# First layer's full self attention: f32 score products in four 32-row bands instead of bf16 parts in stacks, with the closing stage inside

## What is computed

```python
def attention(x, w_qkv, b_qkv, w_o, b_o):       # 16 heads, dh = 8, no mask
    qkv = x @ w_qkv + b_qkv
    q, k, v = jnp.split(qkv, 3, axis=-1)
    ...
    scores = jnp.einsum('bqhd,bkhd->bhqk', q, k) / jnp.sqrt(jnp.float32(dh))
    probs = jax.nn.softmax(scores, axis=-1)
    ctx = jnp.einsum('bhqk,bkhd->bqhd', probs, v).reshape(B, T, D)
    return ctx @ w_o + b_o
h = x + attention(layer_norm(x, ln1_w, ln1_b), w_qkv, b_qkv, w_o, b_o)
return h + moe_ff(layer_norm(h, ln2_w, ln2_b), w_gate, w1, b1, w2, b2)
```

## Time and profile before

| | us |
|---|---|
| median of 3 runs | 2156.8 |
| profiled execution | 2162.13 |
| its span | 2160.4 |
| TensorE busy | 1709.4 (79%) |
| VectorE busy | 1297.4 (60%) |
| ScalarE busy | 1013.1 (47%) |
| mean granted TensorE clock | 0.893 |

### The profile page before, as it was taken

The page is one execution under the profiler, slowest core; times in us unless marked ns, Lnnn a source line. Parts: engine busy times, 40 slices in busy tenths (PEclk is TensorE's granted clock), DMA queues, the critical chain, the costliest instruction groups (busy, mean ns, idle before and its releaser), DMA issues. The chain is left out here.

```text
span 2160.4 us, 32545 instructions
## 1 busy us (share of the span) xinstructions
PE 1709.4 (79%) x9889; PEld 969.6 (45%) x9942; DVE 1297.4 (60%) x4106; ACT 1013.1 (47%) x1938; POOL 153.7 (7%) x280
## 2 busy tenths in 40 slices
PE   4187877287416955969999499999999989989997
PEld 2044444154201321336777344454545455656664
DVE  7388896565735844733333487767676745764445
ACT  3188884075103633643334167667576643332221
POOL 2000000300100000010000100000000002330000
PEclk8599998598756987988999799999999998998999
DMA  1533400340152124001000110000000000000000
GB/s 56 81 40 40 44 0 3 57 56 8 41 81 31 20 26 44 1 3 40 20 20 10 39 40 1 1 1 1 1 1 1 1 1 3 1 1 23 22 15 27
DMA packets 57630, 48.74 MB, mean 23 GB/s; under 512 B 12692, under 2 KB 53048, under 8 KB 57528
## 3 DMA queue, kind: packets, MB, share of 16 engines
q1 hardware_dynamic: 57527, 47.45, 13.8%
HBM read 38.30 MB, written 8.91 MB: 22 GB/s over the span
## 5 line engine op out<-in xcount | busy, mean ns | idle before, releaser
L557 DVE TENSOR_REDUCE c_NM<-ps_t 128x1 f32<-128x512 f32 x256 | 169.9, 688 | 96.9 <-PE ps_t L437 95.2
L1556 ACT ACTIVATE d_PT<-ps_t 128x512 f32<-128x512 f32 x256 | 150.5, 589 | 105.8 <-PE ps_t L1472 105.8
L1547 ACT ACTIVATE d_PR<-d_PR,d_NM 128x512 f32<-128x512 f32 x256 | 183.9, 718 | 32.9 <-DVE d_NM L1618 32.9
L437 PE MATMUL ps_t<-KX,QX 96*128 (+1 forms) x256 | 108.3, 428 | 105.6 <-DVE c_IB L575 46.8
L619 ACT ACTIVATE c_PT<-ps_s 128x1024 f32<-128x1024 f32 x128 | 130.4, 1024 | 126.6 <-PE ps_s L460 124.5
L2358 DVE SCALAR_TENSOR_TENSOR X<-ps_t,GATE,X 128x128 f32<-128x128 f32 x272 | 76.6, 344 | 185.3 <-PE ps_t L2283 185.3
L762 ACT ACTIVATE a_PR<-a_PR,a_NM 128x128 f32<-128x128 f32 (+3 forms) x256 | 129.8, 555 | 78.8 <-DVE a_NM L743 78.8
L1618 DVE CUSTOM_DVE_ANT_0 d_PR<-ps_s,d_BH 128x512 f32<-128x512 f32 x256 | 165.4, 683 | 0.3 <-PE ps_s L1463 0.2
L672 PE MATMUL ps_t<-ident,a_PR 128*128 128x128 f32 x640 | 117.9, 295 | 49.8 <-ACT a_PT L686 37.4
L2320 ACT ACTIVATE f_HT<-ps_s,f_BE 128x512 f32<-128x512 f32 x128 | 87.9, 687 | 128.6 <-PE ps_s L2273 127.8
L1463 PE MATMUL ps_s<-d_K,d_Q 64*128 64x512 f32 x512 | 145.0, 644 | 1.3 <-DVE d_NM L1618 1.3
(11 more groups left out here) (330 smaller groups left out, 2989.8 us busy)
## 6 DMA issues: line engine op xcount, KB each, us to landing
QX<-split_parts SPq DMA_DIRECT2D x108, 128.0 KB
KX<-split_parts SPq DMA_DIRECT2D x72, 128.0 KB
f_W<-in_L_ffn_w SPq DMA_DIRECT2D x16, 256.0 KB, 3.1
split_parts<-a_PARTS SPq DMA_DIRECT2D x8, 384.0 KB, 10.3
split_parts<-c_PARTS SPq DMA_DIRECT2D x8, 384.0 KB, 10.6
g_W<-in_L_ffn_w SPq DMA_DIRECT2D x24, 128.0 KB, 2.3
split_parts<-b_PARTS SPq DMA_DIRECT2D x4, 384.0 KB, 10.7
X<-in_x SPq DMA_DIRECT2D x4, 256.0 KB
```

Source lines behind the costliest of these rows:

```text
L437: nc.tensor.matmul(c.ps_t[:, i % 2, :], QX[0:SROWS, bass.ds(head, 1), qt * P:(qt + 1) * P], KX[0:SROWS, bass.ds(head, 1), :], start=True, ...
L557: nc.vector.tensor_reduce(NM[:, qt, j:j + 1], c.ps_t[:, i % 2, :], AX.X, ALU.max, negate=True).then_inc(maxed, 1)
L1547: nc.scalar.activation(PR[:, n % RING, e, :], PR[:, n % RING, e, :], ACT.Exp, scale=-1.0, bias=NM[:, n % RING, e:e + 1], accum_out=DEN[:, ...
L1556: nc.scalar.activation(PT[:, g % 2, e, :, qt * P:(qt + 1) * P], c.ps_t[:, e, :].rearrange("p (k q) -> p k q", q=P), ACT.Copy).then_inc(tak ...
```

## The change

The three blocks become one. The bf16 parts, their way through HBM, the stacks and the split of the maxima are gone. `NarrowWeights` loads all weights of the stage in seven DMAs, issued at the start of the closing block of the cross attention before it (`early`).

- Weights: queries' and keys' weights are copied into padded tiles in which each head has 32 columns (8 of its own, the rest zero), so that a projection of a group of four heads puts head j on rows 32j to 32j+7, its band. Row 32j+8 of the keys is one (from the bias), and the same row of the queries takes the negated maxima.
- Projections: queries and keys of step t+2 are computed in f32 within step t, values of the next batch in the first step of a batch, all through the one bank ps_f, whose users follow one another in the order of `shared_uses`.
- Scores: `score` contracts 8 rows of a band in f32 into one of three banks; VectorE takes the maxima, 24 tiles ahead of the rest. The 16 columns of maxima of a step are turned by one transpose, copied by ScalarE to 16 rows and written by four DMAs to the four rows 32j+8 of the queries.
- `score_by_key` contracts 9 rows of a band into one of three other banks, with the head two bands away from that of the `score` beside it; exp takes 512 columns; the four value products follow every fourth tile.
- The closing stage of a batch (context turned, output product, residual, statistics, normalised, turned back) runs inside the next batch's steps.
- All loops are written out; there is no hardware loop. The ones written into KX (L1141) are gone.

The diff, cut to its core; the lines removed from the old function are those printed above.

```diff
-def narrow_full_attention(c, tag, own, QX, KX, scratch, s_qx):
...
+    def load(self, sp, w, b, wo, bo, ln_w, ln_b):
+        sp.dma_start(self.W[:, :, :], w.rearrange("p (i n) -> p i n", i=3)).then_inc(self.loaded, 16)
+        sp.dma_start(self.BROW[:, :, :].rearrange("a i n -> a (i n)"), row(b, 1)).then_inc(self.loaded, 16)
+        sp.dma_start(self.BV[:, :], row(b[2 * P:3 * P])).then_inc(self.loaded, 16)
+        sp.dma_start(self.WO[:, :], wo).then_inc(self.loaded, 16)
+        sp.dma_start(self.BO[:, :], row(bo)).then_inc(self.loaded, 16)
+        sp.dma_start(self.WB[:, 0:1], col(ln_w)).then_inc(self.loaded, 16)
+        sp.dma_start(self.WB[:, 1:2], col(ln_b)).then_inc(self.loaded, 16)
...
+def narrow_full_attention(c, tag, weights, early=None):
...
+    MAXIMA_LEAD = 24
+    ALL = STEPS * TILES
+    MBANKS = [c.ps_s[:, i, :] for i in range(3)]
+    KBANKS = [c.ps_s[:, 3, :], c.ps_t[:, 0, :], c.ps_t[:, 1, :]]
+    PTS = 3
...
+        def shared_uses():
+
+            order = [("q", 0), ("k", 0), ("v", 0), ("q", 1), ("k", 1), ("n", 0)]
+            for t in range(STEPS):
+                b, g = divmod(t, GROUPS)
+                if t + 2 < STEPS:
+                    order += [("q", t + 2), ("k", t + 2)]
+                if t:
+                    order.append(("t", t - 1))
+                if t + 1 < STEPS:
+                    order.append(("n", t + 1))
+                if g == 0 and b + 1 < B:
+                    order.append(("v", b + 1))
+                if g and b:
+                    order.append((("1", "o", "x")[g - 1], b - 1))
+            order += [("t", STEPS - 1), ("1", B - 1), ("o", B - 1), ("x", B - 1)]
+            return dict(zip(order[1:], order))
...
+                for u in range(STEPS):
+                    sp.wait_ge(s_nm, u + 1)
                     for j in range(GH):
+                        sp.dma_start(QG[CW * j + HD8:CW * j + HD8 + 1, u % 3, :].rearrange("a (k q) -> a k q", q=P),
+                                     NMT[j * QT:(j + 1) * QT, u % 2, :]).then_inc(s_row, 16)
+                sp.wait_ge(s_row, rows_all * STEPS)
...
+                nc.gpsimd.memset(WP[:, :, :, :], 0.0).then_inc(s_zero, 1)
+                nc.gpsimd.memset(BP[:, :, :, :], 0.0).then_inc(s_zero, 1)
+                nc.gpsimd.memset(ONE[:, :], 1.0).then_inc(s_zero, 1)
+                pool.wait_ge(s_zero, 2)
+                nc.gpsimd.memset(BP[:, 1, :, HD8:HD8 + 1], 1.0).then_inc(s_zero, 1)
+                nc.gpsimd.memset(VG[:, :, :, :, :], 1.0).then_inc(s_zero, 1)
...
+                def queries(u):
+                    shared_bank_free(pe, ("q", u))
+                    nc.tensor.matmul(c.ps_f[:, :], padded(0, u % GROUPS), columns(u // GROUPS), start=True,
+                                     stop=True).then_inc(s_q, 1)
...
+                def score(m):
+                    u, i = divmod(m, TILES)
+                    qt, j = divmod(i, GH)
+                    if i == 0:
+                        pe.wait_ge(s_qout, u + 1)
+                        pe.wait_ge(s_kout, u + 1)
+                    if m >= 3:
+                        pe.wait_ge(s_max, m - 2)
+                    nc.tensor.matmul(MBANKS[m % 3], QG[head(j, HD8), u % 3, qt * P:(qt + 1) * P], KG[head(j, HD8), u % 3, :],
+                                     start=True, stop=True).then_inc(s_m, 1)
+
+                def turn_maxima(u):
+                    pe.wait_ge(s_max, TILES * (u + 1))
+                    shared_bank_free(pe, ("n", u))
+                    nc.tensor.transpose(c.ps_f[0:TILES, 0:P], NM[:, u % 2, :, :].rearrange("p h q -> p (h q)"),
+                                        c.ident[:, :]).then_inc(s_nt, 1)
+
+                def score_by_key(m):
+                    t, i = divmod(m, TILES)
+                    kt, j = divmod(i, GH)
+                    j = (j + 2) % GH
+                    if i == 0:
+                        pe.wait_ge(s_row, rows_all * (t + 1))
+                    if m >= 3:
+                        pe.wait_ge(s_exp, m - 2)
+                    nc.tensor.matmul(KBANKS[m % 3], KG[head(j, HD8 + 1), t % 3, kt * P:(kt + 1) * P],
+                                     QG[head(j, HD8 + 1), t % 3, :], start=True, stop=True).then_inc(s_st, 1)
+
+                def value_products(w):
+                    t, kt = divmod(w, QT)
+                    b, g = divmod(t, GROUPS)
+                    pe.wait_ge(s_exp, GH * (w + 1))
+                    if kt == 0:
+                        pe.wait_ge(s_vout, b + 1)
+                        if t:
+                            pe.wait_ge(s_ct, t)
                     for j in range(GH):
+                        mm = nc.tensor.matmul(c.ps_v[head(j, CW), :], VG[:, b % 2, kt, g * GH + j, :], PT[:, w % PTS, j, :],
+                                              start=(kt == 0), stop=(kt == QT - 1))
+                    mm.then_inc(s_pv, 1)
...
+                pe.wait_ge(s_pad, 4)
+                bias_columns()
+                queries(0)
+                keys(0)
+                values(0)
+                queries(1)
+                keys(1)
+                for m in range(MAXIMA_LEAD):
+                    score(m)
+                turn_maxima(0)
+                for m in range(ALL):
+                    t, i = divmod(m, TILES)
+                    b, g = divmod(t, GROUPS)
+                    if m + MAXIMA_LEAD < ALL:
+                        score(m + MAXIMA_LEAD)
+                    score_by_key(m)
+                    if i % GH == GH - 1 and m >= TILES // 2 - 1:
+                        w = m // GH - 1
+                        value_products(w)
+                    if i == 0 and t + 2 < STEPS:
+                        queries(t + 2)
+                    if i == 4 and t + 2 < STEPS:
+                        keys(t + 2)
+                    if i == 7 and t:
+                        turn_heads(t - 1)
+                    if i == 9 and t + 1 < STEPS:
+                        turn_maxima(t + 1)
+                    if i == 13:
+                        if g == 0 and b + 1 < B:
+                            values(b + 1)
+                        if g == 1 and b:
+                            turn_context(b - 1)
+                        if g == 2 and b:
+                            output(b - 1)
+                        if g == 3 and b:
+                            back(b - 1)
+                value_products(STEPS * QT - 1)
+                turn_heads(STEPS - 1)
+                turn_context(B - 1)
+                output(B - 1)
+                back(B - 1)
...
+                def exp(m):
+                    t, i = divmod(m, TILES)
+                    w, j = m // GH, (i % GH + 2) % GH
+                    act.wait_ge(s_st, m + 1)
+                    if i % GH == 0 and w >= PTS:
+                        act.wait_ge(s_pv, w - PTS + 1)
+                    nc.scalar.activation(PT[:, w % PTS, j, :], KBANKS[m % 3], ACT.Exp).then_inc(s_exp, 1)
+
+                def maxima_out(u):
+                    act.wait_ge(s_nt, u + 1)
+                    if u >= 2:
+                        act.wait_ge(s_row, rows_all * (u - 1))
+                    nc.scalar.activation(NMT[:, u % 2, :], c.ps_f[0:TILES, 0:P], ACT.Copy).then_inc(s_nm, 1)
...
+                for m in range(ALL):
+                    t, i = divmod(m, TILES)
+                    b, g = divmod(t, GROUPS)
+                    exp(m)
+                    if i == 1 and t + 2 < STEPS:
+                        queries_out(t + 2)
+                    if i == 5 and t:
+                        heads_out(t - 1)
+                    if i == 10 and t + 1 < STEPS:
+                        maxima_out(t + 1)
+                    if i == 14 and g == 1 and b:
+                        context_out(b - 1)
+                    if i == 14 and g == 3 and b:
+                        columns_out(b - 1)
...
+                def maximum(m):
+                    u, i = divmod(m, TILES)
+                    qt, j = divmod(i, GH)
+                    dve.wait_ge(s_m, m + 1)
+                    if i == 0 and u >= 2:
+                        dve.wait_ge(s_nt, u - 1)
+                    nc.vector.tensor_reduce(NM[:, u % 2, j, qt:qt + 1], MBANKS[m % 3], AX.X, ALU.max,
+                                            negate=True).then_inc(s_max, 1)
...
+                for m in range(MAXIMA_LEAD):
+                    maximum(m)
+                for m in range(ALL):
+                    t, i = divmod(m, TILES)
+                    b, g = divmod(t, GROUPS)
+                    if m + MAXIMA_LEAD < ALL:
+                        maximum(m + MAXIMA_LEAD)
+                    if i == 5 and t + 2 < STEPS:
+                        keys_out(t + 2)
+                    if i == 8 and t:
+                        normalise(t - 1)
+                    if i == 14 and g == 0 and b + 1 < B:
+                        values_out(b + 1)
+                    if i == 14 and g == 2 and b:
+                        residual(b - 1)
+                    if i == 15 and g == 2 and b:
```

(52 more changed lines are left out.)

400 lines of the change are left out of this document (209 added, 191 removed).

## The result

The changed kernel takes 2343.9 us (median of 4 runs, 2341.9 to 2348.3), the kernel before in the same comparison 2156.1 us: a ratio of 1.088, interval 1.084 to 1.093. It is 188 us slower. The forecast was 2123 us and faster; the time lies outside the range, near the second rival's 2390, the one in which the clock stays low, and which had a chance of 0.12.

A forecast was written before the change was run, and what follows sets the result against it. TensorE, nearly full, was taken to bound the kernel. Loads 3.3, start 17, maxima ahead 24.6, steps 313.1 and end 13.8 sum to 371.8 against 404.8 us: 33 less, 2156.8 to 2123 us; range 2045 to 2200.

The forecast's parts named there:

- second rival: TensorE in the changed stage: clock stays at half, a step of 37 us, total 2390 us; chance 0.12.
- plain round: Four tiles on TensorE without a projection block: eight score products in four bands, then value products, 4.1 us.
- Steps: Steps of 16 tiles in the changed stage: 20.1 us for each of 13, 313.1 us for all.
- first rival: Score products on TensorE overlap only two deep: 5.05 us a round, 24 us a step, total 2185; chance 0.20.
- third rival: Queries, keys and turns hide in TensorE's wait for S0's bank: 16.4 us a step, total 2064; chance 0.16.
- Start and lead: Stage start with padding and five projections, 17 us, then 24 maxima ahead, 24.6 us; first exp about 42 us after the barrier.
- the padding: Stage start: weights padded and bias columns, 6.5 us taken, between 0.9 and 10.
- The maxima ahead: Before the steps: 24 maxima, a turn and four row copies, 21.6 us plus 3 for low clock, 24.6.
- the end: Stage end: last exp and value products, heads, output product, then the last batch's closing to the last columns: 13.8 us.
- Early loads: Seven loads on SP's queue in front of the cross attention's closing block delay it by 3.3 us.
- Row copies hidden: Each step's four row copies of maxima land at 9.2 us, before next K0 at 9.5; upper bound 1.6 us a step.
- GpSimd's memset priced at nothing: Cross attention's projections: dropping the ones written into the key stack frees POOL, where nobody waited for it; no gain.

The follow-up runs named there:

- two small moves: Changed kernel with 32 rows, queries and keys blocks each one tile later, VectorE's normalise one tile earlier: 2081.6 us, ratio 0.966.

## Why the prediction was wrong

The step that failed is the clock. The sum prices the rounds of all steps at the full clock (4.1 us for a plain round, 20.1 a step) and sets aside the second rival, "the clock stays low", with a chance of 0.12. That rival's mechanism was right, and it was taken for a side case. The argument against it was that "from 682 on the same products with value products between got 1.00, and those are here too, and gaps are short". The products there were not the same: they used 96 and 128 rows of the array, the new ones 8 and 9 in each of four bands. The prediction had that fact in the sentence before ("here 8 or 9 rows are used") and let busy time and gaps outweigh it. The runs show that gaps were not it (96% busy at 0.52) and rows were (0.98 with 32, all else the same). The price of the rival was near: 37 us a step and 2390, measured 33.3 and 2344. In the step from 769.81 to 802.86 us the rounds with a projection take 9.6 us each (5.0 and 5.5 with 32 rows), but the third and the fourth only 6.9 (5.3 and 4.0). Why these grew by less than the products did, no run separates.

The rest of the sum can be held against the kernel with 32 rows, which has the change at the full clock: 2119.5 us against 2123 (or 43.5 us below the kernel before in its own comparison, 2163.0, where 33 were forecast). That this is so near is partly luck: the stage took 10 us more than forecast, and what comes ahead of it 9 us less for a reason that the prediction had put at nothing.

- Steps: 19.5 us measured, 20.1 forecast. Right, and so are the rounds and blocks in the timeline.
- Bands two deep (first rival): wrong, they go four deep, with a wait of their own each. The Trainium skill (TensorE: Matmul & The Clock Gate, "The mechanism" in its part on packing) has matmuls start and end strictly in program order; the trace disagrees: the four products of 804.57 are over after 1.1 us, and with each behind the first half of the one ahead of it they would take 5 x 0.43 = 2.2 us. When products do share a band, the two-deep price nearly comes out (24.7 us a step for 24), and there too the starts are not in the order of the program.
- Projections hide (third rival): no in the order as changed, yes after two small moves (17.0 us a step, 16.4 forecast for it).
- Start and lead: 17 + 24.6 = 42 us forecast, 55 measured to the first exp (551.3 to 606.5). The first score starts at 576.8, 25.5 us after the barrier, where 17 were forecast: the padding takes 11.9 us of it (6.5 forecast, for which there was no row) and the projections 13.6 (10.6). The maxima ahead take 29.7 us (24.6). All five projections run at the clock of 0.50, not only the first, and VectorE's two copies of the weights end 0.15 us behind a memset of GpSimd, as these lines of the changed kernel show:

```profile
553.52 3.50 POOL L533 MEMSET c_VG<- 128x4096 f32 x1
553.70 3.47 DVE L822 COPY c_WP<-c_W 128x128 f32<-128x128 f32 x2 [4.37 <-POOL c_BP L532]
```

  The whole stage with 32 rows is 378.8 us (549.7 to 928.5) where 368.5 were forecast (371.8 less the 3.3 for the loads, which lie ahead of it). This miss is the largest of the sum, 13 us; the steps and the end make 3 of it good.
- Early loads: 3.3 forecast, 3.2 measured by moving them back. Right.
- Row copies hidden: right; K0 waited for them once, 2.0 us.
- GpSimd's memset priced at nothing "where nobody waited for it": wrong by 9 us. No wait in the list names GpSimd, because VectorE did not wait on a semaphore: its instruction was long. What the list of the kernel before has is ScalarE behind it, once 10.2 us for VectorE's parts.

## What to carry to other kernels

Before few rows of the array take the place of many, look for a stretch of the profile with products of that height and read its granted clock; full busy time at the old height did not foretell the clock at the new one here. If a packed product is short of rows, using the whole band with zeros costs no instruction, and was worth 224 us here. And look in each group for the instruction that is many times its own usual length: a wait can hide inside a duration.

## What was unexpected of the hardware

- The granted clock followed the rows in use: 0.52, 0.51, 0.94 and 0.98 for 8 and 9, 16, 24 and 32 rows of each band, with all else equal. The added rows held zeros. It was 0.69 with the value products doubled. With 32 rows in the maxima's products alone it was 0.72. What rule the chip applies is not known from these runs.
- The low state held for all of the 500 us although TensorE was at work for 96% of them; the slices behind the stage read 7 to 9 tenths, as they did before the change.
- A cast of VectorE of 0.43 us took 9.37 and 9.52 us beside a memset of GpSimd of 13.75 us that writes another tensor, and ended 0.27 and 0.28 us behind it. Two copies of f32 ended with a memset in the same way (L822, above; not tried without it). The Trainium skill (SBUF — State Buffer, "Who interferes with whom") says that an instruction of VectorE in a two-port mode and one of GpSimd take turns on a shared pair of ports, and that whoever comes second waits for the whole of the other. The trace agrees in the cast's end; that the cast runs in such a mode it does not show.
